# Adding routed expert rows into the residual by accumulating gathers, with their weights applied at the PSUM exit

## The reference

```
x = x + tanh(g_xattn[0]) * sparse_adjacency(ctx_512, layernorm(x))
# mixture of experts: E = 8, K = 2, I = 352
scores  = softmax(xn @ gate_w.T);  topk_w, topk_idx = top_k(scores, 2)
topk_w  = topk_w / sum(topk_w)
y       = sum_k topk_w[k] * expert[topk_idx[k]](xn)      # silu(xn@w1)*(xn@w3) @ w2
x = x + tanh(g_ffn[0]) * (y + shared_expert(xn))
x = x + tanh(g_xattn[1]) * attention(layernorm(x), ctx_512, ctx_512)   # 32 heads of 16
x = x + tanh(g_ffn[1]) * mx_ffn(layernorm(x))            # MXFP8-rounded FFN, 2048 wide
```

## Time and profile before

| | us |
|---|---|
| median of 3 runs | 1863.89 (1862.64 to 1864.75) |
| the profiled execution, its own time | 1867.28 |
| span of its trace | 1865.5 |
| PE busy | 1512.8 (81%) |
| DVE busy | 1321.0 (71%) |
| ACT busy | 739.6 (40%) |
| POOL busy | 467.6 (25%) |

### The profile page before, as it was taken

How to read it: one execution, slowest core, us unless ns; L and a number is a source line. 1 busy time by engine, 2 the same in 40 slices (tenths; PEclk the granted TensorE clock), 3 DMA queues, 4 the chain that set the end, 5 groups by cost and what they waited for, 6 DMA issues and landing times.

```text
span 1865.5 us, 24234 instructions
## 1 busy us (share of the span) xinstructions
PE 1512.8 (81%) x8186; PEld 726.5 (39%) x8186; DVE 1321.0 (71%) x2502; ACT 739.6 (40%) x1060; POOL 467.6 (25%) x438
## 2 busy tenths in 40 slices
PE   2268585792888988348888888989899999999998
PEld 1134343451555555202222222222345444444444
DVE  7887576737699998698887878886555555555555
ACT  5253435222444544305665656657212222222221
POOL 4211121100566666430000000000132323323222
PEclk8589788996999999758999999999999999999999
DMA  5211121113355554452220210212500000000000
GB/s 162 76 30 58 49 64 58 40 46 105 119 161 175 181 168 154 136 135 46 50 53 2 36 22 0 52 23 46 113 1 0 22 0 0 22 0 0 23 11 12
DMA packets 115036, 114.33 MB, mean 61 GB/s; under 512 B 59448, under 2 KB 87352, under 8 KB 114944
## 3 DMA queue, kind: packets, MB, share of 16 engines
q1 hardware_dynamic: 109184, 94.29, 18.3%
q0 software_dynamic: 5760, 18.88, 3.7%
HBM read 59.53 MB, written 31.46 MB: 49 GB/s over the span
## 4 chain that ended last, share of the span: by engine, by line
PE 56%; DVE 30%; DMA 5%; issue 5%; ACT 3%; POOL 1%; SPq 1%; DVEq 0%; ACTq 0%; POOLq 0%
PE PS L1909 17%; PE PS L1932 9%; PE PS L810 6%; PE PS L1384 6%; DVE WORK L1509 6%; PE PS L1363 5%; PE PS L825 4%; PE PS L1372 3%; DVE WORK L1751 2%; DVE WORK L1769 2%; DVE WORK L1752 2%; PE PS L1922 1%; DMA WORK<-in_L_ffn_up_w_dram 1%; DMA WORK<-in_L_ffn_down_w_dram 1%; DVE WORK L1743 1%
## 5 line engine op out<-in xcount | busy, mean ns | idle before, releaser
L1509 DVE TENSOR_REDUCE WORK<-PS 128x1 f32<-128x512 f32 x512 | 326.3, 686 | 71.5 <-PE PS L1363 68.5
L1909 PE MATMUL PS<-BIG 128*128 128x512 f16 x1536 | 342.5, 383 | 8.7 <-DVE BIG L1987 4.6
L1291 ACT ACTIVATE BIG<-PS 128x1024 f32<-128x1024 f32 x256 | 261.6, 1025 | 165.1 <-PE PS L1372 162.8
L1363 PE MATMUL PS<-BIG 128*128 128x512 f16 x512 | 205.5, 404 | 68.9 <-DVE WORK L1509 45.3
L1909 PEld LDWEIGHTS PS<-BIG 128*128 128x128 f16 x1536 | 151.5, 99 | 191.1 <-issue 10.2
L810 PE MATMUL PS<-BIG,WORK 128*128 (+1 forms) x1152 | 184.8, 318 | 4.8 <-DVE WORK L845 4.8
L1932 PE MATMUL PS<-BIG 128*128 128x512 f16 x768 | 173.8, 379 | 1.8 <-DVE BIG L2007 1.8
L1845 ACT ACTIVATE WORK<-PS 128x512 f32<-128x512 f32 x64 | 38.2, 597 | 306.7 <-PE PS L1909 306.7
L1372 PE MATMUL PS<-BIG 128*128 128x512 f16 x512 | 155.3, 387 | 0.1
L1384 PE MATMUL PS<-BIG 128*32 128x512 f32 x1024 | 138.8, 614 | 9.9 <-issue 6.9
L1363 PEld LDWEIGHTS PS<-BIG 128*128 128x128 f16 x512 | 50.1, 98 | 247.2 <-DVE WORK L1509 200.0
(11 more groups left out here) (242 smaller groups left out, 2300.1 us busy)
## 6 DMA issues: line engine op xcount, KB each, us to landing
wdq_scratch<-WORK SPq DMA_DIRECT2D x48, 256.0 KB
WORK<-in_L_ffn_w_dram SPq DMA_DIRECT2D x32, 352.0 KB, 3.6
y_scratch<-WORK SPq DMA_DIRECT2D x40, 256.0 KB, 2.9
BIG<-BIG SPq DMA_DIRECT2D x96, 64.0 KB, 2.3
X<-in_x_dram SPq DMA_DIRECT2D x4, 1024.0 KB, 9.0
WORK<-in_L_ffn_w_dram SPq DMA_DIRECT2D x16, 256.0 KB, 2.7
WORK<-in_L_ffn_gate_w_dram SPq DMA_DIRECT2D x16, 256.0 KB, 3.4
WORK<-in_L_ffn_up_w_dram SPq DMA_DIRECT2D x16, 256.0 KB, 3.6
```

Of the source, the lines that this page charges most:

```text
L1291: nc.scalar.activation(PB[:, tp, 2 * h:2 * h + 2, :], BPAIR[h % 2], ACT.Exp, scale=SOFT_SCALE).then_inc(exp_ok, 1)
L1363: nc.tensor.matmul(ABANK[i], QS[:, g * HG + h, r * P:(r + 1) * P], KA[:, g, :], start=True, stop=True).then_inc(a_mm, 1)
L1509: v.tensor_reduce(MXU[:, g % 2, c:c + 1], ABANK[i], AX_X, ALU.max, negate=True).then_inc(max_ok, 1)
L1909: ins = nc.tensor.matmul(bank[b], fxT[:, p, a, k * P:(k + 1) * P], w[:, c, l, k, :], start=(i == 0), stop=(i == 3 * KD - 1))
```

## The change

ScalarE's copy of a slot from PSUM takes a scale for each partition, `WSL[:, i]`, the weight and gate of the pair in that place. To get `WSL`, VectorE computes `CW` earlier, splits it into two f16 parts times 1024 (`CWS`), multiplies `tile_hot` with each (`tile_w`), and TensorE sums 64 more matmuls into bank 3. The product with the row's number now goes to a table of its own, `tile_tok`. Each of the 32 gathers from `y_scratch` adds its rows into `X[:, t, :]` itself (`compute_op=ALU.add`). They go in groups of four row tiles, first choice of the four, then second choice; the second waits until the first has landed. `combine(t)` keeps the wait and the statistics. The clearing of `KK` stands behind the first eight gathers and no longer waits for `QW.lo_ok`. In stage `c` GpSimd waits for `zeros_ok` before it fills `V`. The buffers `mgath` are gone.

```diff
-        mgath = [carve(WORK, f"mgath{i}", at, [P, 2, D]) for i, at in enumerate((28928, 33024, 10240, 14336))]
+        tile_tok = carve(WORK, "tile_tok", 14848, [P, E2 * TT, SLOTS], F16)
+        tile_w = [carve(WORK, f"tile_w{l}", at, [P, E2 * TT, SLOTS], F16) for l, at in enumerate((18944, 14848))]
+        CWS = carve(WORK, "CWS", 28544, [P, 2, E2, TT], F16)
+        WSL = carve(WORK, "WSL", 28672, [P, SLOTS])
+        W_UP = 1024.0
+        AHEAD = 4
+        mg_in = [[sem(f"mg_in{k}{p}") for p in range(AHEAD)] for k in range(2)]
@@ b_gpsimd
             pool.wait_ge(MO.y_mm, SLOTS)
-            pool.wait_ge(QW.lo_ok, UNITS)
-            nc.gpsimd.memset(KK...[32:64, :], 0.0).then_inc(zeros_ok, 1)
             for p in range(2):
                 pool.wait_ge(yst[p], 16 * (SLOTS // 2) + 16)
-            for t in range(TT):
-                if t >= len(mgath):
-                    pool.wait_ge(mg_used, t - len(mgath) + 1)
-                for k in range(2):
-                    nc.gpsimd.indirect_dma_start(mgath[t % len(mgath)][:, k, :], None, y_dram, ...)
+            def add_rows(k, t):
+                if k or t >= AHEAD:
+                    pool.wait_ge(mg_in[0][t % AHEAD], 16 * (t // AHEAD + k))
+                if k and t >= AHEAD:
+                    pool.wait_ge(mg_in[1][t % AHEAD], 16 * (t // AHEAD))
+                nc.gpsimd.indirect_dma_start(X[:, t, :], None, y_dram,
+                                             bass.IndirectOffsetOnAxis(ap=POS[:, k, t:t + 1], axis=0),
+                                             compute_op=ALU.add).then_inc(mg_in[k][t % AHEAD], 16)
+            for t0 in range(0, TT, AHEAD):
+                for k in range(2):
+                    for t in range(t0, t0 + AHEAD):
+                        add_rows(k, t)
+                if t0 == 0:
+                    nc.gpsimd.memset(KK...[32:64, :], 0.0).then_inc(zeros_ok, 1)
@@ b_scalar
-                nc.scalar.activation(yo[:, p, :], bank[6 + p][:, :], ACT.Copy)
+                nc.scalar.activation(yo[:, p, :], bank[6 + p][:, :], ACT.Copy, scale=WSL[:, i:i + 1])
@@ b_tensor
+            pe.wait_ge(hot_ok, 2)
+            for i in range(E2 * TT):
+                for l in range(2):
+                    ins = nc.tensor.matmul(bank[3][:, 0:SLOTS], row_hot[:, i, :], tile_w[l][:, i, :], ...)
+            ins.then_inc(map_mm, 1)
@@ b_vector
-            v.tensor_copy(POS, POSF).then_inc(pos_ok, 1)
+            link(v.tensor_copy(POS, POSF))
             ...
             v.tensor_copy(IDX, bank[2][:, 0:SLOTS]).then_inc(idx_ok, 1)
-            fast_lo(dve, 9, E - 1, range(2))
-            for p in range(2):
-                link(v.memset(HOME.hid[:, p, I:KI * P], 0.0))
             dve.wait_ge(e12_ok, 1)
             link(v.tensor_scalar(CW[:, :, 0], CW[:, :, 1], 1.0, None, ALU.add))
             link(v.reciprocal(CW[:, :, 0], CW[:, :, 0]))
             link(v.tensor_tensor(CW[:, :, 1], CW[:, :, 1], CW[:, :, 0], ALU.mult))
-            link(v.tensor_scalar(CW, CW, GATES[:, 7:8], None, ALU.mult))
-            fast_lo(dve, 9, E - 1, range(2, NCH))
+            link(v.tensor_scalar(CWS[:, 0], cw, W_UP, None, ALU.mult))
+            link(v.scalar_tensor_tensor(CWS[:, 1], cw, W_UP, CWS[:, 0], ALU.mult, ALU.subtract))
+            for l in range(2):
+                link(v.tensor_tensor(tile_w[l], tile_hot, CWS[:, l]...to_broadcast([P, E2 * TT, SLOTS]), ALU.mult))
+            v.nop().then_inc(hot_ok, 1)
+            fast_lo(dve, 9, E - 1, range(3))
+            dve.wait_ge(map_mm, 2)
+            link(v.tensor_scalar(WSL, bank[3][:, 0:SLOTS], GATES[:, 7:8], 1.0 / W_UP, ALU.mult, ALU.mult))
+            for p in range(2):
+                link(v.memset(HOME.hid[:, p, I:KI * P], 0.0))
+            fast_lo(dve, 9, E - 1, range(3, NCH))
@@ c_gpsimd
+            pool.wait_ge(zeros_ok, 3)
@@ c_vector, combine(t)
-                dve.wait_ge(mg_in[t % len(mgath)], 32 * (t // len(mgath) + 1))
-                for k in range(2):
-                    ins = v.scalar_tensor_tensor(X[:, t, :], mgath[t % len(mgath)][:, k, :], CW[:, t, k:k + 1], X[:, t, :], ...)
-                ...
-                dve.wait_ge(mg_used, t + 1)
+                dve.wait_ge(mg_in[1][t % AHEAD], 16 * (t // AHEAD + 1))
                 v.bn_stats(bnst_c[:, t, :], X[:, t, :]).then_inc(row_st, 1)
```

More of the change, by code:

```diff
@@ L767, in build @@
         rank_mm = sem("rank_mm")
-        pos_ok = sem("pos_ok")
         eid_ok = sem("eid_ok")
@@ L775, in build @@
         yst = [sem("yst0"), sem("yst1")]
-        mg_in = [sem(f"mg_in{p}") for p in range(len(mgath))]
-        mg_used = sem("mg_used")
+        AHEAD = 4
+        mg_in = [[sem(f"mg_in{k}{p}") for p in range(AHEAD)] for k in range(2)]
         class Unit:
@@ L917, in b_gpsimd @@
             pool.wait_ge(MO.y_mm, SLOTS)
-            pool.wait_ge(QW.lo_ok, UNITS)
-            nc.gpsimd.memset(KK.rearrange("p a b c -> p (a b c)")[32:64, :].bitcast(F32), 0.0).then_inc(zeros_ok, 1)
             for p in range(2):
                 pool.wait_ge(yst[p], 16 * (SLOTS // 2) + 16)
-            for t in range(TT):
-                if t >= len(mgath):
-                    pool.wait_ge(mg_used, t - len(mgath) + 1)
+            def add_rows(k, t):
[7 more added lines that the diff above has]
+            for t0 in range(0, TT, AHEAD):
                 for k in range(2):
-                    nc.gpsimd.indirect_dma_start(mgath[t % len(mgath)][:, k, :], None, y_dram,
-                                                 bass.IndirectOffsetOnAxis(ap=POS[:, k, t:t + 1], axis=0)
-                                                 ).then_inc(mg_in[t % len(mgath)], 16)
+                    for t in range(t0, t0 + AHEAD):
+                        add_rows(k, t)
+                if t0 == 0:
+                    nc.gpsimd.memset(KK.rearrange("p a b c -> p (a b c)")[32:64, :].bitcast(F32), 0.0).then_inc(zeros_ok, 1)
         def b_scalar(act):
@@ L958, in y_out @@
                     act.wait_ge(yst[p], (i - p) * 8 + 16)
-                nc.scalar.activation(yo[:, p, :], bank[6 + p][:, :], ACT.Copy).then_inc(MO.y_out, 1)
+                nc.scalar.activation(yo[:, p, :], bank[6 + p][:, :], ACT.Copy, scale=WSL[:, i:i + 1]).then_inc(MO.y_out, 1)
             for i in range(SLOTS):
@@ L978, in b_tensor @@
             for i in range(E2 * TT):
-                ins = nc.tensor.matmul(bank[2][:, 0:SLOTS], row_hot[:, i, :], tile_hot[:, i, :],
+                ins = nc.tensor.matmul(bank[2][:, 0:SLOTS], row_hot[:, i, :], tile_tok[:, i, :],
                                        start=(i == 0), stop=(i == E2 * TT - 1))
+            ins.then_inc(map_mm, 1)
+            pe.wait_ge(hot_ok, 2)
+            for i in range(E2 * TT):
+                for l in range(2):
+                    ins = nc.tensor.matmul(bank[3][:, 0:SLOTS], row_hot[:, i, :], tile_w[l][:, i, :],
+                                           start=(i == 0 and l == 0), stop=(i == E2 * TT - 1 and l == 1))
             ins.then_inc(map_mm, 1)
@@ L1059, in b_vector @@
             for k in range(2):
-                half = tile_hot[:, k * TT:(k + 1) * TT, :]
-                link(v.tensor_tensor(half, half, TOK[:, :].unsqueeze(2).to_broadcast([P, TT, SLOTS]), ALU.mult))
+                half = slice(k * TT, (k + 1) * TT)
+                link(v.tensor_tensor(tile_tok[:, half, :], tile_hot[:, half, :],
+                                     TOK[:, :].unsqueeze(2).to_broadcast([P, TT, SLOTS]), ALU.mult))
             v.nop().then_inc(hot_ok, 1)
-            v.tensor_copy(POS, POSF).then_inc(pos_ok, 1)
+            link(v.tensor_copy(POS, POSF))
             fast_lo(dve, 8, E - 2, range(2 * NBUF, NCH))
@@ L1080, in b_vector @@
             link(v.tensor_tensor(CW[:, :, 1], CW[:, :, 1], CW[:, :, 0], ALU.mult))
-            link(v.tensor_scalar(CW, CW, GATES[:, 7:8], None, ALU.mult))
-            fast_lo(dve, 9, E - 1, range(2, NCH))
+            cw = CW.rearrange("p t k -> p k t")
+            link(v.tensor_scalar(CWS[:, 0], cw, W_UP, None, ALU.mult))
+            link(v.scalar_tensor_tensor(CWS[:, 1], cw, W_UP, CWS[:, 0], ALU.mult, ALU.subtract))
+            for l in range(2):
+                link(v.tensor_tensor(tile_w[l], tile_hot,
+                                     CWS[:, l].rearrange("p a b -> p (a b)").unsqueeze(2).to_broadcast([P, E2 * TT, SLOTS]),
+                                     ALU.mult))
+            v.nop().then_inc(hot_ok, 1)
[5 more added lines that the diff above has]
+            fast_lo(dve, 9, E - 1, range(3, NCH))
             dve_lo(dve, MO, HOME, 0, 0)
```

## The result

Slower. The changed kernel's median is 1865.65 us (1861.47 to 1871.09, 20 runs), beside 1862.14 us (1858.13 to 1864.91, 20 runs) for the kernel before: the ratio is 1.0021, with a 95% interval of 1.0012 to 1.0029, or about 4 us. The forecast was 1857 us, 7 us faster; the median lies within the range of 1853 to 1884, on the other side of no change.

The account below looks back on a forecast made before the run. TensorE and VectorE hold most of the chain, VectorE being the limit at the change of stage. Terms +1.9 + 0.3 - 0.85 - 10.4 + 2 = -7.0 us: 1860.3 profiled, 1857 median, range 1853 to 1884.

Parts of the forecast that it names:

- routing: Ahead of the last expert's first fast_lo: VectorE's added work for the weights starts the slots late, +1.9 us.
- exit: ScalarE's scaled copy from PSUM: 0 to 0.18 us more each, mostly hidden; two slots at the stage's end, +0.3 us.
- front of the new stage: Change of stage up to SP's first copy: transposes without additions between them let it start at 799.3, -0.85 us.
- crowding: SP's first six copies share the DMA engines with gathers: between 0 and 4.4 us, taken as +2.
- the 32 maxima: VectorE at the change of stage: seven pairs of additions drop out from between the maxima, -10.4 us.
- Price of an accumulating gather: Gathers into X: the period p at which they land, taken as 1.5 us, with GpSimd's 1.25 as lower bound.
- GpSimd's issue becomes the bound: Rival, chance 0.08: an adding instruction takes twice its 0.95 us on GpSimd, period 2.2, kernel +4.5 us.
- The adds are bound by the DMA engines: Rival, chance 0.30: p above 1.76 makes the kernel slower; +3 us at 1.86, +12 at 2.15, +21 at 2.4.
- second limit: Change of stage: combine(15) needs the last gather, then six maxima and statistics; end at 834.8 us at the latest.
- first limit: Change of stage: VectorE's path through the thirteenth gather, transposes and 32 maxima, ending at 834.1 us.
- Comes 33 us after its first one ... so it is covered: SP's small copy with the maxima, behind its other copies, is hidden by VectorE's moments of 4.6 us, costing nothing.
- the case p = 1.25: Gathers landing at GpSimd's old issue period, the forecast's fast end: sum -10 us, 1853 to 1854 us.

Follow-up runs that it names:

- x_plain: The changed kernel with its 32 gathers into X as plain ones that overwrite, the addition left out; 1853.21 us, ratio 0.9961 to the kernel before.
- x_route: The kernel before with the new routing and scaled PSUM exit alone, VectorE's additions kept with weight one; 1862.69 us, ratio 1.0009 to before.
- x_match: The changed kernel with plain gathers, no addition, each behind a GpSimd clearing of 766 columns, so 1.87 us apart; 1861.27 us, ratio 0.9996 to before.
- x_defer: The changed kernel with combine(4) to combine(7) moved behind the last lo_q; 1862.84 us, ratio 1.0007 to before.
- x_best: The changed kernel with tiles 0 to 3 gathered plainly and added by VectorE, plus four edits of order and KK clearing; 1854.18 us, 0.9958 to before.
- x_sp: The changed kernel with SP's small copy of the maxima behind six groups of copies, not all 48 copies; 1865.87 us, ratio 1.0017 to before.

## Why the prediction was wrong, step by step

The runs make a ladder from before to after, each step from ratios times 1862 us: routing and exit +1.7; gathers into `X` in place of VectorE's additions, at the old pace (x_plain against x_route), -8.9; GpSimd's pace from 1.25 to 1.87 us (x_match against x_plain) +6.5; the dearer transfer (after against x_match) +4.7. The sum is +4.0, as it must be, since each rung starts where the last ends. The intervals make a rung uncertain by 1.7 us (the first) to 3.3; the traces from T give the last three as -8.5, +7.4 and +5.3.

From T the terms compare as follows:

| us | forecast | measured, after against before |
|---|---|---|
| SP's first copy (front of the new stage) | -0.85 | +7.5 |
| from there to the first maximum (crowding) | +2 | +4.1 |
| the 32 maxima | -10.4 | -11.0 |
| from their end to the next maximum | 0 | +1.9 |
| sum | -9.25 | +2.4 (the columns are rounded) |

**The step that failed is "Price of an accumulating gather"**: "I take 1.5". It is 1.86 us (1.555 for the instruction and 0.30 between two), and GpSimd sets it, with the engines close behind. The step took GpSimd's 1.25 as a bound from below, as if the instruction that issues a gather took the same time with an addition. It takes 0.61 us more. The thirteenth gather landed at 796.7 and not at 787.45. Of these 9.2 us, 1.5 are the start of the first (765.67 against 764.2), half of it because T lies 0.8 us later than before and most of the rest because GpSimd starts 0.8 us after the last store has landed, where I took 0.2; 4.7 the eight instructions up to the ninth gather (783.98 against 777.8, less the start); 1.4 the four periods behind it, of 1.86 and not 1.5; and 1.6 the landing (5.26 against 3.65). `lo_ctx` and the transposes followed it as forecast, and so SP's first copy.

**The engines' share was under-priced too.** Of the nearest rows I chose the loads under a full queue, 0.75 and so 1.5; doubling the gather's own 0.93 was right (1.86 forecast by that row, 1.78 measured, against 0.89 for plain ones at the same pace). By the rule of the Trainium skill's page "Collectives: The Full Stack" (section "The bandwidth ceiling: the fold count and why AG ≠ RS ≠ AR"), two reads for each chunk of a reducing transfer and the addition itself free, the cost doubles; the trace agrees. So both limits lie together: 1.78 of engines under 1.86 of GpSimd. By this estimate a faster issue alone would gain at most 0.08 us for each gather; no run tried one.

**The rivals.** "GpSimd's issue becomes the bound" (0.08) named the mechanism; its estimate of a doubled instruction was above the 1.55 measured, and its +4.5 came from the last gather, so that it lies near the measured +4 by luck. "The adds are bound by the DMA engines" had +3 at p = 1.86, and the measured is +4, but again by another way: its second limit, the last gather for `combine(15)`, did not bind in after (tiles 9 to 15 waited for nothing). In x_defer, with the first limit out of the way, tiles 8, 9 and 12 waited for their gathers, and tile 15 still did not. Both together had 0.38, and against GpSimd stood only that nothing in the trace said that the time goes by addresses. Nothing said that it doesn't either.

**"Comes 33 us after its first one ... so it is covered" failed.** Under the adds SP's 48 copies take 40.2 us, and the small copy behind them comes 1.9 us after VectorE could go on. The crowding of the first six, taken at 2 us, was 4.1, and against plain gathers at the same pace it is 2.6. The upper end of 4.4 does not follow from what is given for it (18 packets behind 0.37 us each would be 6.7), so that 4.1 lies under it says little. Nor does the rival's +21 at p = 2.4 follow from its own formula, which gives +20.

**Right:** the 32 maxima; the transposes at 2.57 to 2.6 us from `lo` to `lo`; the memset, which put the ninth gather off by 3.4 us and which the moments of after did not wait for; the products for the weights (3.0 forecast, 3.02) and the direction of routing, +1.9 forecast, +1.4 in the traces. There the first chunk was 1.8 us later behind the cast to `IDX` (4.41 against 2.64 us), near to forecast; of this 0.3 did not reach the transposes, so it is not quite paid in full. With the exit the forecast was +2.2 and the ratios say 3.5 ± 1.7. The exit itself is 0.09 us a copy, in the middle of the 0 to 0.18 given. x_plain, the case p = 1.25, was put at -10 and measured -7.3; the 1.3 between 3.5 and 2.2 may be half of the gap, but it is smaller than its own interval.

**Open:** why the adding instruction takes longer. The page counts the packets of GpSimd's queue:

```profile
q0 software_dynamic: 7808, 18.88, 4.9%
```

That is 2048 more than the 5760 of before, 64 for each of the 32 gathers (144 and not 80), and would fit more descriptors to write. The Trainium skill's page "DMA: Bandwidth & Descriptors" (section "SWDGE vs HWDGE vs iDMA") has GpSimd's cores compute descriptors in software, a pair for each operation. No run here varies their number. Open too is how the gain of x_best divides between its five edits.

## What to carry to other kernels

Before work is moved from an engine into a transfer, price the instruction that issues the transfer as a changed instruction, and look for whoever else uses the transfer engines in that stretch: the adds here doubled the load, and an unrelated queue of small copies lost 9 us to it. Count from the first transfer to the first consumer at the slower pace: twelve issues at 0.61 us more cost 7.3 us ahead of SP's first copy, where the 14 additions taken from VectorE had cost 10.5. Use such transfers where their consumer comes late (tiles 4 to 15), and leave to the idle engine what is wanted at once.

## What the runs showed of the hardware

- An indirect gather of 128 rows of 2 KB takes GpSimd 0.949 us when it writes and 1.555 us when it adds. From its start to its landing are 3.4 us (x_match, one every 1.87 us) and 6.0 us (after), medians over all 32; the 16 DMA engines are busy for 0.89 and 1.78 us.
- SP's copies of SBUF to SBUF take 0.6 us of its queue, and up to 1.76 us under the adds. Plain gathers at either pace did not lengthen them (31.4 us for 48), though in x_plain at 797 to 808 us gathers and copies together kept the engines busy for 95% of the time. The copies of 64 KB issued there landed after 4.8 us (median), against 2.6 for those of before at 790 to 835 us: what shared engines delayed there was the landing and not the queue.
- ScalarE's copy of 128 x 512 from PSUM takes 597 ns plain and 686 ns with a scale per partition.
- A product of 1280 columns, f16 with f16, took 1.5 us on VectorE with one factor broadcast, as the comparison of f32 with f32 did.
- The first 48 matmuls of the FFN took 10.5 to 13.4 us over the profiled executions. The mean granted clock of their first 4 us was 0.50 (half of 2.4 GHz) in before and x_sp, which took 13.4, and 1.00 in after, x_match and x_defer, which took 10.5. This alone moves a single execution by 2.9 us, almost as much as the whole change.
